# Layer 0 of a graph network: quads of four consecutive rows, and the rows of x fetched by as many node blocks as each span needs

## What is computed

```python
# layer 0
gathered = x[dst] * edge_weight[:, None]
pre_embed = segment_sum(gathered, src, num_segments=8192)
x = layernorm(x + pre_embed @ W.T)
# layer 1
summand = tensor_product(x[src], edge_attr_9, [w0, w1, w2, w3, w4])   # per edge
x = layernorm(x + segment_sum(summand, dst, num_segments=8192) / sqrt(10))
```

## Time and profile before

| what | value |
|---|---|
| median of 3 runs | 4366.64 us (4366.34 to 4369.26) |
| the profiled execution, its own time | 4366.83 us |
| its span, from the first to the last instruction | 4365.0 us |
| setup and sort | about 0 to 493 us |
| loop of layer 0 | about 511 to 1727 us |
| norm, then layer 1 | about 1729 to 4365 us |
| TensorE, VectorE, ScalarE, GpSimd busy | 71, 50, 30, 66% of the span |
| mean granted TensorE clock | 0.782 |

### The profile page before, as it was taken

How to read it: one execution, slowest core, us unless ns; L and a number is a source line. 1 busy time by engine, 2 the same in 40 slices (tenths; PEclk the granted TensorE clock), 3 DMA queues, 4 the chain that set the end, 5 groups by cost and what they waited for, 6 DMA issues and landing times.

```text
span 4365.0 us, 70523 instructions
## 1 busy us (share of the span) xinstructions
PE 3101.0 (71%) x21792; PEld 2730.4 (63%) x21794; DVE 2180.7 (50%) x4636; ACT 1298.2 (30%) x2113; POOL 2886.9 (66%) x3027
## 2 busy tenths in 40 slices
PE   2210399999999999576767676666667666766776
PEld 1000399999999999465656555555555555655565
DVE  8999766666676766533232333333332323233443
ACT  5454466666666665201010010101010100101121
POOL 5200277777776765577777777777777777777776
PEclk6555699999999999577777777777777777777777
DMA  1000111111111112222222222222222222222232
GB/s 55 15 0 19 55 51 48 48 49 48 50 49 49 48 49 65 88 56 56 57 56 56 57 56 57 56 56 56 56 56 57 56 56 57 56 57 61 80 86 63
DMA packets 111885, 234.04 MB, mean 54 GB/s; under 512 B 52081, under 2 KB 52225, under 8 KB 110673
## 3 DMA queue, kind: packets, MB, share of 16 engines
q0 software_dynamic: 96560, 200.21, 17.2%
q1 hardware_dynamic: 10658, 24.72, 1.8%
q10 hardware_dynamic: 4608, 8.39, 0.5%
HBM read 218.42 MB, written 8.40 MB: 52 GB/s over the span
## 4 chain that ended last, share of the span: by engine, by line
POOL 35%; issue 12%; PE 8%; DMA 2%; DVE 1%; POOLq 1%; ACT 0%; DVEq 0%; ACTq 0%
POOL feat L1512 35%; PE mixed L1642 4%; PE quad L1627 3%; DMA feat<-x,ids 2%; DVE group L1738 1%; PE attr_t L1593 1%; PE quad L1620 0%; POOLq L1509 0%; POOLq L1508 0%; POOLq L1505 0%; POOLq L1510 0%; ACT ids L1553 0%; DVEq L1738 0%; PE y L1636 0%; ACT z_last L1568 0%
## 5 line engine op out<-in xcount | busy, mean ns | idle before, releaser
L1512 POOL DMA_INDIRECT feat<-x,ids x2048 | 1937.3, 946 | 636.5 <-issue 620.9
L1071 POOL DMA_INDIRECT l_feat<-in_x,id_of x896 | 851.1, 950 | 672.6 <-ACT w_of L767 334.9
L1738 DVE TENSOR_TENSOR group<-group,quad 128x504 f32 (+1 forms) x512 | 347.9, 679 | 1723.7 <-PE quad L1627 1689.6
L1627 PE MATMUL quad<-attr_hot,feat 128*128 128x144 f32 x4096 | 808.3, 353 | 494.8 <-DMA feat<-x,ids 494.8
L1627 PEld LDWEIGHTS quad<-attr_hot,feat 128*128 128x128 f32 x4096 | 678.8, 235 | 634.9 <-DMA feat<-x,ids 382.6
L1642 PE MATMUL mixed<-group,mix 128*128 128x192 f32 x2304 | 674.5, 477 | 235.3 <-DVE group L1738 235.3
L1642 PEld LDWEIGHTS mixed<-group,mix 128*128 128x128 f32 x2304 | 634.2, 299 | 278.4 <-issue 246.9
L1553 ACT CAST ids<-src_col 128x8 int32 (+1 forms) x256 | 50.5, 197 | 2178.3 <-PE quad L1627 2178.3
L1155 PE MATMUL got<-x_near,far_w 128*128 128x128 bf16 x6912 | 479.1, 220 | 1.9 <-ACT far_keys L785 1.3
L1155 PEld LDWEIGHTS got<-x_near,far_w 128*128 128x128 bf16 x6912 | 435.3, 98 | 2.3 <-issue 2.2
L1717 DVE TENSOR_TENSOR attr_hot<-hot,attr_t 128x1152 f32<-128x1152 f32 x256 | 346.4, 1353 | 9.0
(11 more groups left out here) (271 smaller groups left out, 3387.7 us busy)
## 6 DMA issues: line engine op xcount, KB each, us to landing
feat<-x,ids POOLq DMA_INDIRECT x2048, 2.5
l_feat<-in_x,id_of POOLq DMA_INDIRECT x896, 2.5
attr_in<-in_edge_attr SPq DMA_DIRECT2D x129, 72.0 KB, 2.2
norm_x<-in_x SPq DMA_DIRECT2D x16, 256.0 KB, 2.6
x<-norm_z ACTq DMA_DIRECT2D x16, 256.0 KB, 2.4
x_t<-x SPq DMA_DIRECT2D x15, 256.0 KB, 3.1
out<-z_t ACTq DMA_DIRECT2D x15, 256.0 KB, 2.1
keys<-far_keys SPq DMA_DIRECT2D x2, 512.0 KB, 3.3
```

Of the source, the lines that this page charges most:

```text
L1071: pool.indirect_dma_start(feat[:, landing % RING, :], None, x, bass.IndirectOffsetOnAxis(ap=id_of[s % 2][:, c:c + 1], axis=0)).then_inc(fe ...
L1512: pool.indirect_dma_start(feat[z][:, t, :], None, x1, bass.IndirectOffsetOnAxis(ap=ids[z][h][:, t % H:t % H + 1], axis=0),).then_inc(feat_ ...
L1627: last = nc.tensor.matmul(bank[:, :, bass.ds(places[t % H], WIN)], feat[z][:, t, :], attr_hot[h][:, t % H, :, :], start=False, stop=(t % Q ...
L1738: nc.vector.tensor_tensor(to, to, quad[:, q, 0:NA * QUAD_WIN].rearrange("p (m n) -> p m n", m=NA), ALU.add).then_inc(quad_added, 1)
```

## The change

Lanes now hold the rows in order, four consecutive rows to a quad, and the constant PART_OF says which quad of rows stands at which quad of lanes. Consecutive rows have neighbouring dst, so a quad has one span, from 8 nodes (the first) to 510 (the last). The 19 quads with the smallest spans are picked. PICKED gives each its place in a group and a kind, which says the node blocks it gets: S one block, D two, U three, M one block and a rest of 42 nodes, T two blocks and such a rest. The picked quads have 30 blocks and 4 rests. 13 tiles a part are gathered, into 13 buffers.

```diff
-FETCHED = ((0, 2, 4, 6, 7), (1, 3, 5, 6))
-GATHERS = ((1, 3, 5), (0, 2, 4, 7))
-RING = 14
+PICKED = ((("S", 0, 1), ("S", 1, 2), ("D", 10, 4), ("T", 16, 5), ("M", 8, 7)),
+          (("S", 2, 1), ("S", 3, 2), ("D", 11, 4), ("T", 17, 5), ("M", 9, 7)),
+          (("S", 4, 1), ("S", 5, 2), ("D", 12, 4), ("D", 13, 5), ("U", 18, 7)),
+          (("S", 6, 1), ("S", 7, 3), ("D", 14, 5), ("U", 15, 7)))
+FETCHED = tuple(tuple(i for _, _, i in picked) for picked in PICKED)
+GATHERS = ((0, 3, 6), (0, 3, 6), (0, 3, 6), (0, 2, 4, 6))
+RING = 13
-SPAN = 288
-REST = SPAN - 2 * P
-CENTER = SPAN // 2
+REST = P // 3
+CENTER = 192
+BLOCKS = {"S": (0,), "M": (1,), "D": (0, 1), "T": (0, 1), "U": (0, 1, 2)}
+RESTED = "MT"
+ROOM = {"S": P, "M": P + REST, "D": 2 * P, "T": 2 * P + REST, "U": 3 * P}
+SHIFT = {"M": P}
...
-    row = np.where(lane % 2 == 0, lane // 2, P - 1 - lane // 2)
+    row = np.array([PART_OF[v // MERGED] * MERGED + v % MERGED for v in lane])
```

In setup, the lower and upper spans give way to one span, compared with the room of its kind:

```diff
-            own, other = lanes[:, 0, :], lanes[:, 1, :]
-            link(nc.vector.tensor_tensor(extent[:], lanes[:, 0:2, 1], lanes[:, 0:2, 0], ALU.subtract))
...
-            link(nc.vector.tensor_tensor(miss[:, 0:1], extent[:, 0:1], extent[:, 1:2], ALU.max))
+            nc.vector.tensor_tensor(extent[:, 1:2], lanes[:, 0, 1:2], lanes[:, 1, 1:2], ALU.max)
+            link(nc.vector.tensor_tensor(extent[:, 0:1], lanes[:, 0, 0:1], lanes[:, 1, 0:1], ALU.min))
+            nc.vector.tensor_tensor(g.span_from[:, 0:1], extent[:, 0:1], g.cst[:, C_SHIFT:C_SHIFT + 1], ALU.subtract)
+            link(nc.vector.tensor_tensor(extent[:, 1:2], extent[:, 1:2], extent[:, 0:1], ALU.subtract))
+            link(nc.vector.tensor_tensor(miss[:, 0:1], extent[:, 1:2], g.cst[:, C_ROOM:C_ROOM + 1], ALU.is_gt))
...
-            link(nc.vector.tensor_scalar(keep_a[:], some[:, 0:1], -1.0, 1.0, ALU.mult, ALU.add))
...
+            nc.vector.tensor_scalar(g.span_from[:, 1:2], g.span_from[:, 0:1], float(CENTER), None, ALU.add)
+            link(nc.vector.tensor_scalar(shown_in[:], g.cst[:, C_IDENT:C_IDENT + P:MERGED], g.span_from[:, 0:1], None,
+                                         ALU.mult))
...
-            for c in range(3):
-                place = g.cst[:, C_PLACE + c:C_PLACE + c + 1]
-                link(nc.vector.tensor_scalar(g.node_f[:, c, :], extents, place, None, ALU.is_le))
-                link(nc.vector.tensor_tensor(g.node_f[:, c, :], g.node_f[:, c, :], deltas, ALU.mult))
-                link(nc.vector.tensor_tensor(g.node_f[:, c, :], g.node_f[:, c, :], firsts, ALU.add))
-                link(nc.vector.tensor_scalar(g.node_f[:, c, :], g.node_f[:, c, :], place, None, ALU.add))
+            for c in range(4):
+                nc.vector.tensor_scalar(g.node_f[:, c, :], pb[:, 1, 0:QUADS], g.cst[:, C_PLACE + c:C_PLACE + c + 1], None,
+                                        ALU.add)
```

In `first_edges`, the rows of x are loaded in 3 batches instead of 5, by block and not by quad. The step that told lower from upper nodes before the loop is gone. In the loop each operation works on the columns that need it:

```diff
-    BATCHES = FILLED // STAGED
+    BATCHES = 3
...
-            link(nc.vector.tensor_scalar(from_lower[:], dst_f, g.pair[:, 1:2], g.pair[:, 2:3], ALU.is_ge, ALU.mult))
...
-            nc.vector.scalar_tensor_tensor(pos[:], dst_f, g.pair[:, 4:5], from_lower[:], ALU.subtract,
-                                           ALU.subtract).then_inc(pos_made, 1)
+            nc.vector.tensor_scalar(pos[:], dst_f, g.span_from[:, 1:2], None, ALU.subtract).then_inc(pos_made, 1)
...
-                nc.scalar.activation(rest_far[:, 0:used], place[z][:, 0:used], ACT.Abs, bias=not_wanted).then_inc(far_made, 1)
+                nc.scalar.activation(rest_far[:, cols], place[z][:, cols], ACT.Abs, bias=not_wanted[which - 2]
+                                     ).then_inc(far_made, 1)
...
-                nc.vector.tensor_scalar(near_hot[z][0][:, 0:used], place[z][:, 0:used], wanted[0], None, ALU.is_equal)
+                nc.vector.tensor_scalar(near_hot[z][0][:, cols[0]], place[z][:, cols[0]], wanted[0], None, ALU.is_equal)
...
-                for m in range(NF[z]):
-                    a = j // 2 * sum(NF) + z * NF[0] + m
-                    to = got[:, m * P:(m + 1) * P]
-                    for c in range(2):
-                        for part in range(3):
-                            nc.tensor.matmul(to, near_hot[z][c][:, m * P:(m + 1) * P], x_near[:, a, 3 * c + part, :],
-                                             start=(c == 0 and part == 0), stop=False)
-                    last = nc.tensor.matmul(to, rest_hot[z][:, m * P:(m + 1) * P], x_rest[:, a, :], start=False,
-                                            stop=True)
+                hots = [*near_hot[z], rest_hot[z]]
+                for m, i in enumerate(FETCHED[j]):
+                    quad = j * GROUP + i
+                    cols = slice(m * P, (m + 1) * P)
+                    products = [(hots[c][:, cols], x_near[:, BLOCK_LIST.index((quad, c)), part, :])
+                                for c in BLOCKS[PLACED[quad]] for part in range(3)]
+                    if quad in REST_LIST:
+                        products.append((rest_hot[z][:, cols], x_rest[:, REST_LIST.index(quad), :]))
+                    for n_done, (hot, rows) in enumerate(products):
+                        last = nc.tensor.matmul(got[:, cols], hot, rows, start=(n_done == 0),
+                                                stop=(n_done == len(products) - 1))
```

More of the change, by code:

```diff
@@ L71 @@
 TURNS = 3
-X_QUADS = [c for c in range(QUADS) if c % GROUP in FETCHED[c // GROUP % 2]]
-FILLED = 20
+PLACED = {j * GROUP + i: kind for j, picked in enumerate(PICKED) for kind, _, i in picked}
+PART_OF = {j * GROUP + i: part for j, picked in enumerate(PICKED) for _, part, i in picked}
+UNPICKED = [k for k in range(QUADS) if k not in PART_OF.values()]
+PART_OF.update(zip([c for c in range(QUADS) if c not in PART_OF], UNPICKED))
+BLOCK_LIST = [(c, k) for c in sorted(PLACED) for k in BLOCKS[PLACED[c]]]
+REST_LIST = [c for c in sorted(PLACED) if PLACED[c] in RESTED]
+BLOCK_SLOTS = 32
 WIN = 16
@@ L144, in constants @@
     spare = lane < 3 * REST
-    for k in range(2):
+    for k in range(3):
         c[:, C_PLACE + k] = k * P + lane
         c[:, C_WANTED + k] = k * P + lane - CENTER
-    c[:, C_PLACE + 2] = np.where(spare, 2 * P + lane % REST, 2 * P)
-    c[:, C_WANTED + 2] = np.where(spare, 2 * P + lane % REST - CENTER, -1000)
+    c[:, C_PLACE + 3] = np.where(spare, 2 * P + lane % REST, 2 * P)
+    c[:, C_WANTED + 3] = np.where(spare, 2 * P + lane % REST - CENTER, -1000)
+    kinds = [PLACED.get(v // MERGED) for v in lane]
+    c[:, C_ROOM] = [ROOM[kind] - 0.5 if kind else 2.0 ** SRC_BITS for kind in kinds]
+    c[:, C_SHIFT] = [SHIFT.get(kind, 0) for kind in kinds]
     return c.astype(np.float32)
@@ L497, in first_edges @@
     PERH = LH * GROUPS
-    USES = PER // 2 * sum(NG) // RING
+    assert sum(NG) == RING and max(GATHERS[-1]) + TURNS >= GROUP
     short = [(RUNS * p, RUNS * k) for p, k in comparators(n // RUNS)]
@@ L610, in group_no, with gather_no, holding, columns @@
             return (wd * PS + ws) * (R * PER) + t * PERH + (hf * (R * PERH) + s * GROUPS + j)
-        def gather_no(s, j):
-            return (s * GROUPS + j) // 2 * sum(NG) + (j % 2) * NG[0]
+        def gather_no(j):
+            return sum(NG[0:j])
+        def holding(j, c):
+            return [m for m, i in enumerate(FETCHED[j]) if c in BLOCKS[PLACED[j * GROUP + i]]]
+        def columns(picked):
+            assert picked == list(range(picked[0], picked[-1] + 1))
+            return slice(picked[0] * P, picked[-1] * P + P)
+        def third(j):
+            rested = [m for m, i in enumerate(FETCHED[j]) if PLACED[j * GROUP + i] in RESTED]
+            assert bool(rested) != bool(holding(j, 2))
+            return (3, columns(rested)) if rested else (2, columns(holding(j, 2)))
+        def share(b, c):
+            at = b * 3 + c
+            return slice(at * STAGED, (at + 1) * STAGED) if at < SHARES else None
+        def loaded(b, c, i):
+            if share(b, c) is None:
+                return 3, REST_LIST[i % len(REST_LIST)]
+            quad, block_no = BLOCK_LIST[((b * 3 + c) * STAGED + i) % len(BLOCK_LIST)]
+            return block_no, quad
         def part_no(wd, ws, hf, t, s):
@@ L697, in split_step @@
             def split_step(b, i):
-                quads = slice(b * STAGED, (b + 1) * STAGED)
                 c, part = i % 3, i // 3
```

142 lines of the change are left out of this document (60 added, 82 removed).

## The result

The changed kernel takes **4263.23 us** (median of 4 runs, 4261.17 to 4264.99) where the kernel before took 4366.60 beside it: ratio **0.976**, 95% interval 0.9745 to 0.9779. The forecast was 4251, its range 4243 to 4283: right in direction and mechanism, 12 us short of the time.

What follows compares the result with a forecast made beforehand. TensorE was taken to bound layer 0's loop. From 4366.83 us, -110.3 for fetch and spread and -5.5 for setup, all else 0, gave 4251 us, 2.65% less; range 4243 to 4283.

Steps and rivals of the forecast that it cites:

- (a): Layer 0's loop, fetch: 94 matmuls a part instead of 126, 32 fewer at 55.6 ns, -1.779 us a part.
- (b): Layer 0's loop, spread of node numbers: one more matmul a part, +0.056 us.
- (d): Gap between last fetch matmul and first sum pass: no growth taken; bound above 0.1 us a group, +26 us.
- (e): Setup before the loops: VectorE's chain of linked small operations gets shorter, -5.5 us, bounds 0 and -7.
- (c): Layer 0's loop, sums: still eight tiles a group, one tile a part fetched instead of gathered, at the same price.
- (f): Sort stage: fewer row gathers, casts and matmuls, none of which VectorE waits for; cost 0 both ways.
- (g): Before the loop: one VectorE operation goes and one gets cheaper, hidden behind ScalarE's copies; cost 0.
- GpSimd second: Layer 0's loop: 13 gathers a part cost 16.5 us against TensorE's 17.20, so GpSimd stays second, 4% to spare.
- (h): Layer 1: unchanged, starts earlier and takes as long.
- the gap grows: Rival, ends of layer 0's groups: gap grows or ScalarE's message is late, half the cut goes, 4306 us; chance 0.08.
- A cut hidden: Rival, layer 0's loop: a copy, comparison, one-hot chain sets the group, only setup's 5.5 us go, 4361; chance 0.02.
- gathers at the sort's price: Rival, layer 0's loop: gathers as slow as in the sort, 1.75 us each with gap, kernel 4609 us; chance 0.02.

## Why the prediction was right, and where it was short

**(a), (b), right to 0.3 us.** 2048 matmuls at 55.6 ns; the runs with 126 matmuls and with no gap give 55.7 to 56.0 ns and 0.428 us a slot. So neither the 98 ns weight load nor a slower stream decides. The Trainium skill, TensorE: Matmul & The Clock Gate, section Back-to-back issue gap, gives about 81 ns for such a stream; this trace does not agree, 55.6 ns with a weight load to each matmul.

**(d) is the step that failed: "I take none, since 28 is the row nearest to 21 to 27".** It took the gap for a matter of the fetch's length and chose the row by that. The fetch's length plays no part (126 and 94 matmuls have the same gaps); the row chosen differed from its neighbour in something else, the kind of the first tile, and in that the change is like the other one. Priced by the earlier trace rows, every group would have had 0.13: half of them had it already, so 128 x 0.1 = +13 us and a forecast of 4264. The gap by slots of the eight in a pass was 0.28, 0.13, 0.03, 0.14, 0.13, 0.13, 0.04, 0.16 before and 0.39, 0.13, 0.13, 0.13, 0.22, 0.13, 0.14, 0.14 after, 11.3 us over 256 slots. The range held it, since the bound above was 26. The load itself takes 0.587 to 0.622 us wherever it stands; the Trainium skill, DMA: Bandwidth & Descriptors, section Latency and other measured facts, names a floor of about 600 ns for it, and the trace agrees.

**(e) right:** -5.9 for -5.5. **(c), ScalarE, VectorE: hidden,** as said: TensorE waits for neither in the loop. **(f), (g) a little short.** The loop starts 4.5 us earlier, not 5.9. VectorE's first reduction behind the sort, before and after, starts 3.93 us earlier, so the sort takes 2.0 us longer, and from there to the loop 0.5 us are given back, where the forecast had neither:

```profile
491.69 2.27 DVE L916 TENSOR_REDUCE l_feat<-far_w 128x16 f32<-128x2048 f32 x1
...
487.76 2.27 DVE L938 TENSOR_REDUCE l_feat<-far_w 128x16 f32<-128x2048 f32 x1
```

VectorE's waits in the sort after the change have three rows that were not there:

```profile
DVE pad L904 <- DVE far_w L927: 0.5, 1, 0.5
DVE pad L904 <- DVE w_row L914: 0.5, 1, 0.5
DVE w_row L927 <- DVE w_row L916: 0.5, 1, 0.5
```

By the profile VectorE waits for itself there, not for a gather or a copy. They are 1.4 of the 2.0 us; the rest is spread over the sort. Six further runs on the changed kernel's sort start the loop at 509.06 to 509.65 us, two on the one of before at 513.44 and 513.94, so the loss is steady; what makes it was not tried and stays open.

**GpSimd second: right, with more cover than forecast.** The interval was put at 1.27 and is 1.25. Its waits for the sums were to fall from 115.3 to some 40 us and fell to 64.6 (560 to 1580 us), since the part is 17.40 us and not 17.20 and 13 gathers take 16.25 us and not 16.5:

```profile
POOL l_feat L1092 <- PE l_pre L1199: 64.6, 105, 0.9
```

**(h)** Layer 1's gathers take what they took, and the stretch behind the loop is 1.0 us longer, in a remainder of 2637:

```profile
L1533 POOL DMA_INDIRECT feat<-x,ids x2048 | 1937.5, 946 | 636.5 <-issue 621.0
```

Of the rivals, "the gap grows" was the right place with a fifth of its size, 11 of 55 us, and for another reason than the one given. A cut hidden, gathers at the sort's price, a loop over 135 passes: none came; the gathers take 0.947 us each.

## What to carry to other kernels

When a short gap stands between two pieces of work of the busiest engine, look at what its queue does there and from which moment, before asking what the engine does: here the queue ran 1.0 us ahead of a stream of short matmuls, so everything that it has to do behind them beyond 1.0 us lies bare, whatever their number. Behind the longer sum passes it was 2.1 us ahead. Put slow steps of the queue (a load of registers, a wait that takes an instruction of its own) where its lead is long, and see that no wait for another engine has eaten the lead: moved by one line it was worth 55 us, half as much as the whole change. And when a price is taken from the nearest row, list in what else the two rows differ. The best version here is the change with the load at the head of the slot, 4208 us; it leaves GpSimd 2% to spare, so the next step must take work from both.

## What the runs showed that I had not expected

- TensorE's queue is 1.0 us ahead of the engine in a stream of 128-column matmuls with their weight loads at clock 1.00, about 18 pairs, in fetches of 21, 27, 28 and 35 alike.
- Behind the sum passes, 0.157 us apart, the queue's lead is 2.1 us in the median (1.7 to 2.3). With 14 gathers, where TensorE waits for them, it falls to as little as 0.64 us.
- A wait that needs an instruction of its own adds 0.11 us to the queue's way to the first sum pass, though nothing is waited for. The order of the tiles alone moves the kernel before by +10.8 us and the changed one by -26.6.
- Without the gap the first pair of sum passes is shorter too, by 0.043 us a slot; the cause is open.
- Gathers of 128 rows keep 1.25 us from one to the next (the median) with GpSimd at 71% and when it is itself the bound (990 us over 792).
